# Second attention: three products placed between the projections of the next head, and the copies of a finished context half placed ahead of the query's

## The reference

```
x = x + 0.5 * ffn0(layernorm(x))           # 1 block, hidden 1024, gelu
x = x + attention0(layernorm(x))           # 16 heads of 16, rope, causal
x = x + 0.5 * ffn0(layernorm(x))
x = x + 0.5 * ffn1(layernorm(x))           # 6 blocks, layernorm between them
x = x + attention1(layernorm(x))           # the stage that is changed
x = x + 0.5 * ffn1(layernorm(x))
```

```
q, k, v = h @ Wq.T, h @ Wk.T, h @ Wv.T
scores  = q @ k.T, masked to the causal half
out     = softmax(scores) @ v, heads side by side, @ Wo.T + bo
```

## Time and profile before

| what | value |
| --- | --- |
| median of 3 runs | 2765.53 us |
| lowest, highest | 2757.81, 2772.41 us |
| the profiled execution | 2771.37 us, its span 2769.5 us |
| PE busy in the span | 2550.3 us (92%) |
| PEld busy | 2123.4 us (77%) |
| DVE busy | 1843.1 us (67%) |
| ACT busy | 1396.5 us (50%) |
| POOL busy | 367.1 us (13%) |

### The profile page before, as it was taken

The page is one execution under the profiler, slowest core; times in us unless marked ns, Lnnn a source line. Parts: engine busy times, 40 slices in busy tenths (PEclk is TensorE's granted clock), DMA queues, the critical chain, the costliest instruction groups (busy, mean ns, idle before and its releaser), DMA issues. The chain is left out here.

```text
span 2769.5 us, 49771 instructions
## 1 busy us (share of the span) xinstructions
PE 2550.3 (92%) x16744; PEld 2123.4 (77%) x16744; DVE 1843.1 (67%) x4018; ACT 1396.5 (50%) x2464; POOL 367.1 (13%) x279
## 2 busy tenths in 40 slices
PE   3985999869899999997999999999999999999999
PEld 3863445448788888886778878788777888888888
DVE  4566676546576777765677767667767666777773
ACT  3430554555455555553555555555555555555553
POOL 1000000010112222212101100100100122222220
PEclk9986789779999999998999999999999999999999
DMA  4026133000000000000000000000000000000000
GB/s 155 0 81 140 25 48 48 2 31 1 31 31 1 30 30 30 0 20 0 20 20 1 19 0 19 19 0 19 19 0 31 31 21 11 31 30 0 30 0 31
DMA packets 18930, 73.28 MB, mean 26 GB/s; under 512 B 3328, under 2 KB 8192, under 8 KB 15616
## 3 DMA queue, kind: packets, MB, share of 16 engines
q1 hardware_dynamic: 18816, 71.78, 9.1%
HBM read 61.02 MB, written 10.49 MB: 26 GB/s over the span
## 5 line engine op out<-in xcount | busy, mean ns | idle before, releaser
L349 PEld LDWEIGHTS ps<-w,hid 128*128 128x128 f32 x5376 | 698.7, 190 | 55.7 <-DVE rb L423 14.5
L349 PE MATMUL ps<-w,hid 128*128 128x256 f32 x5376 | 719.2, 284 | 2.1 <-DVE rb L423 1.5
L318 PE MATMUL ps<-xT,w 128*128 (+1 forms) x2688 | 704.1, 398 | 0.0
L500 DVE TENSOR_TENSOR hid<-gel,hid 128x512 fp32r<-128x512 f32 x448 | 400.9, 905 | 363.3 <-ACT hid L390 354.9
L384 ACT ACTIVATE gel<-ps,b 128x512 f32<-128x512 f32 x448 | 306.9, 686 | 556.8 <-issue 543.8
L318 PEld LDWEIGHTS ps<-xT,w 128*128 128x128 f32 x2688 | 479.7, 190 | 79.4
L390 ACT ACTIVATE hid<-gel 128x512 fp32r<-128x512 f32 x448 | 272.9, 622 | 0.0
L835 PE MATMUL ps<-pT,v_sb 128*128 128x512 f32 (+3 forms) x1152 | 261.5, 358 | 1.6 <-DVE pT L952 1.6
L809 PE MATMUL ps<-k_sb,q_sb 128*128 128x512 f32 (+3 forms) x1152 | 251.5, 351 | 1.5 <-DVE q_sb L969 1.4
L1401 DVE TENSOR_REDUCE nmx<-ps 128x1 f32<-128x512 f32 (+3 forms) x384 | 196.1, 552 | 84.3 <-PE ps L1272 63.4
L941 DVE TENSOR_REDUCE negmax<-ps 128x1 f32<-128x128 f32 (+7 forms) x256 | 192.3, 752 | 77.3 <-PE ps L812 76.1
(11 more groups left out here) (118 smaller groups left out, 2909.5 us busy)
## 6 DMA issues: line engine op xcount, KB each, us to landing
wraw<-in_wffn SPq DMA_DIRECT2D x12, 2048.0 KB, 7.8
wraw<-in_w_a SPq DMA_DIRECT2D x8, 1280.0 KB, 5.4
qk_dram<-rope_hl SPq DMA_DIRECT2D x16, 512.0 KB, 3.0
xT<-qk_dram SPq DMA_DIRECT2D x60, 128.0 KB, 8.3
qk_own<-qk_dram SPq DMA_DIRECT2D x36, 128.0 KB, 6.4
xb<-in_wffn SPq DMA_DIRECT2D x2, 2048.0 KB, 12.6
x<-in_x SPq DMA_DIRECT2D x4, 512.0 KB, 5.5
rot<-in_rot SPq DMA_DIRECT2D x1, 2048.0 KB, 18.7
```

What stands on the lines that cost most here:

```text
L318: last = nc.tensor.matmul(ps[:, HPS + j % 4, :], w[par][:, wp, 0, k * HIDDEN + j * PART:k * HIDDEN + (j + 1) * PART], xT[:, xp, k, bass.ds ...
L349: last = nc.tensor.matmul(y_ps[:, t, :], hid[:, hp, j % 4, t * PART:(t + 1) * PART], w[par][:, wp, 1, j * DIM:(j + 1) * DIM], start=j == 0 ...
L500: nc.vector.tensor_tensor(hid[:, 1, j % 4, :], gel[:, j % 4, :], hid[:, 0, j % 4, :].bitcast(f32), ALU.subtract).then_inc(low_done, 1)
```

## The change

Three strings of the table are edited, and nothing else. On PE, m1, m2 and m3 no longer stand behind q0' but between k1', v0', v1' and q0', one after each; and m4 stands ahead of q1' instead of behind it. On ACT and on DVE, c0 stands ahead of q0' instead of behind it.

```diff
         ORDER = dict(
-            pe=("s6 wo3- s7 k0' m0 t2 t3 k1' v0' v1' q0' m1 m2 m3 t4 t5 q1' m4 t6 t7 m5 "
+            pe=("s6 wo3- s7 k0' m0 t2 t3 k1' m1 v0' m2 v1' m3 q0' t4 t5 m4 q1' t6 t7 m5 "
                "s0' s1' wo0 t8 m6 t9 wo1 t10 m7 s2' t11 w0' s3' m8 m9 m10 m11 s4' w1' "
                "s5' t0' t1' wo2"),
             act=("high10- w0 high11- exp2 exp3 c1- w1 exp4 high0 exp5 high1 k0' exp6 high2 "
-               "k1' high3 exp7 q0' c0 high4 high5 q1' high6 high7 exp0' high8 high9 "
+               "k1' high3 exp7 c0 q0' high4 high5 q1' high6 high7 exp0' high8 high9 "
                "exp1'"),
             dve=("q1 low6- inv4- inv5- max0 low7- wo0- low8- max1 low9- wo1- low10- inv6- "
                "max2 max3 low11- w0 max4 c1- inv7- w1 max5 wo2- low0 max6 wo3- low1 k0' "
-               "k1' max7 v0' low2 low3 inv0 v1' inv1 inv2 q0' inv3 c0 low4 low5"),
+               "k1' max7 v0' low2 low3 inv0 v1' inv1 inv2 c0 q0' inv3 low4 low5"),
         )
```

## The result

The changed kernel takes 2829.85 us (median of 4, 2823.79 to 2836.27); the kernel before takes 2761.67 us (median of 4, 2752.68 to 2772.41). The ratio is 1.0242, 95% interval 1.0207 to 1.0278: 2.4% slower. The profiled execution has a span of 2834.5 us, 65.0 over that of before. All ratios, also those of the experiments, compare executions in the same state of the clock; one execution of the kernel with the values projected earlier, 3157 us at a mean granted clock of 0.74, is left out of its ratio.

The account below looks back on a forecast made before the run. TensorE's string of work was taken as the path, without slack, so each wait lengthens the stage. 54.1 (ordinary) + 9.1 (group starts) + 5.4 (last two heads) = 68.6 us over the 2765.53 median gave 2834.1 us, range 2805 to 2852.

Parts of the forecast that it names:

- The ordinary passage: From one head to the next, 22 times: s0' starts 2.46 us later in each, 54.1 us in all.
- m2's wait: Ordinary passage, TensorE ahead of m2: a new wait of 0.61 us for low2, since q0' no longer stands as cover.
- m4's wait: Ordinary passage, TensorE ahead of m4: 1.81 us in place of 0.30, since low4 stands behind q0' on DVE.
- the cover of q1': Ordinary passage, ahead of m4: q1' (1.28 us) stood there as cover before; now it is queued behind the waiting m4.
- Group starts: Passages where a group starts, 7 times: s0' comes 1.30 us later in each, 9.1 us in all.
- The last two passages: Ahead of the last two heads: m2 waits for low2, q0' starts later, s0' 2.72 us later each, 5.4 us.
- The low end: Rival, all passages: q0' does not hold up low4 and s0' does not wait; 40.4 us, 2806; chance 0.08.
- the weight loads going ahead: Rival, at m2 and m4: weight loads go ahead of both waits, saving 11.2 us; 2823; chance 0.05.
- the delay spreads: Rival, each passage: exponentials, maxima or next products wait up to 0.5 us further, 15.5 us more; 2850; chance 0.10.
- The faster case: Rival: m1 to m3 hidden in the projections' waits, early c0 removes the wait at m4; 2749; chance 0.03.
- a net of no change: Rival, whole kernel: gains at group starts and losses in ordinary passages cancel; 2766; chance 0.03.

## Where the prediction was right and where it was wrong

**The sum** was 68.6 us, the medians differ by 68.2, the stage by 65.6. The time forecast, 2834.1 us, is 4 us over the 2829.85 measured, since the kernel before came out 3.9 us under the 2765.53 that the forecast started from.

**The ordinary passage** was put at 2.46 us and is 2.18 from t2 to wo0 (10.78, before 8.60) in 21 of them; that makes 45.8 us. m2's wait came as drawn from the last head, 0.70 us where 0.61 was put. Three terms were a little large: m2 and m3 take 0.69 us ahead of q0', not 0.80; inv3 holds low4 up by 0.07 us, not 0.15; and behind its wait s0' and its followers up to wo0 take 0.87 us instead of 0.99, which wins back 0.12. m4's wait is 1.51, not 1.81: t4 and t5 take 1.02 us ahead of it where 0.82 was put, and the way from q0' to m4's weights is 3.80 us where 3.91 was put. One reading was loose: the old wait of 0.30 us ahead of m4 stands in 18 ordinary passages and 6 group starts, and not in the first group, whose ordinary passages go from 8.48 to 10.70 us.

**One of the 22 was not ordinary**, and the prediction did not see it. Ahead of the last head but two DVE first does the statistics of the next stage (L452, 2.70 us), and TensorE waits 2.36 us for a low part in both kernels. In the changed one this follows:

```profile
2144.60 1.52 PEld L835 LDWEIGHTS ps<-pT,v_sb 128*128 128x128 f32 x6 [2.23 <-DVE pT L952]
2146.00 2.25 PEld L846 LDWEIGHTS ps<-xT,w_kvq 128*128 128x128 f32 x6
```

m2 waits 2.23 us instead of 0.70, and q0' takes 2.25 us instead of 1.23. The passage from t2 to wo0 was 12.36 us at a granted clock of 0.86 and is 16.86 at 0.80, a loss of 4.50.

**Why m4 waits** is the step that was half wrong. The prediction had q0' holding up low4, and took the last head's 1.26 us for a low end. The run with low4 ahead of q0' shows 1.28, and the run with m4 moved alone shows 1.50 with no q0' in the way. The main cause is the other thing that the prediction named, the cover of q1' that is gone; q0' ahead of low4 adds 0.23, where the two ends of the prediction left 0.55. Nor is the last head's 1.26 the work of c0 alone: without c0 in the way t4's own path through ACT and DVE takes nearly as long, as the 1.28 shows.

**Group starts** were put at 1.30 us and lose 1.10 (18.43 against 17.33), 7.7 us. m2 behind v0' waits 1.55 us, as said, and v1' comes 0.63 later.

**The last two passages** were put at 2.72 and lose 3.66 and 3.90 (t2 to wo0: 15.10 and 15.33 against 11.44 and 11.43), 7.6 us instead of 5.4. The step that failed here is that durations stay what they were. After m2's wait of 2.67 us the clock fell, and the six matmuls of q0' took 2.02 us instead of 1.24. This is the timeline of PEld in the changed kernel there:

```profile
2177.76 2.02 PEld L846 LDWEIGHTS ps<-xT,w_kvq 128*128 128x128 f32 x6
```

And these are its busy times in the stretch ahead of that and the one around it, with the granted clock third from the end:

```profile
2170.00:2177.00 7.00, 4.24 (x25) 3.07 (x23) 4.58 (x9) 2.90 (x7) 0.00 (x0) 1.00 0.00 0
2177.00:2183.00 6.00, 5.04 (x21) 4.11 (x22) 2.84 (x10) 3.26 (x6) 0.00 (x0) 0.72 0.00 0
```

Added up, 45.8 + 4.5 + 7.7 + 7.6 = 65.6 us, the whole of the stage. The terms that were too large and those that were left out, the clock and the passage that was not ordinary, nearly cancel: that the total is closer than its parts is luck.

**The rivals.** The low end (2806) and the weight loads going ahead (2823) did not happen: the load of m2 and of m4 starts after the wait in every row above. That the delay spreads did not happen either: behind s0' the timelines of before and after agree. The faster case fails at m2's wait, where it was said to be decided, and a net of no change fails on both kinds of passage.

## What to carry to other kernels

In an order written by hand for an engine that is never idle, a step covers the wait of another, so before moving it count what is left between each result and its next reader: here some 3.1 us from a projection's first load until its bank is free, and some 2.3 us from the first transpose of a key tile to the product that reads it. A filler must be ready when it is reached; one whose operand stands behind the same copies as the wait it should fill only adds to it. Where waits come from one bank used in a row, taking a user out of the row gained 0.8%, while filling the gaps in place with m1 to m3 lost 1.05% by themselves and 2.4% with the rest of the change.

## What was not expected of the hardware

The granted clock does not answer to the sum of the waits alone. The changed kernel idles TensorE for 0.70 and 1.51 us in 21 of 22 ordinary passages and keeps 1.00. With 0.70 and 2.10 us, in one execution, it fell to half for parts of 16 passages that keep it in the changed kernel: relative to the changed kernel the waits themselves account for 18 of the 41.6 us that the stage grew, which leaves about 24 to the clock. Behind m2's waits of 2.23 and 2.67 us near the end it fell as well, and in the kernel before it fell behind the wait of 2.36 us. That kernel bears single waits of 1.91 us with 1.28 and 1.29 behind them at full clock. Nor do the waits alone decide: ahead of the last head but one, with waits of 0.70 and 1.71 us, the kernel before kept 1.00 and the one with the values projected earlier fell to 0.87. Which passages lose the clock stays open. An edit that makes the waits a little longer can so cost more than its waits.
